# A four-layer graph network: the attention stage on pairs of tiles, with the cast and the subtract moved between GpSimd and VectorE

## The chip, the core and the metric

One core of one Trainium2 chip runs the whole program in one launch. The metric is the device time of that launch in microseconds. The profile names the engines: PE (TensorE matmul), PEld (its weight loads), DVE (VectorE), ACT (ScalarE), POOL (GpSimd), SP (the queue that issues most transfers).

## The reference

x is 4096 x 128 and adj 4096 x 4096, of zeros and ones and symmetric, both float32. Four layers follow one another, each on `h = relu(layernorm(x))` and added to x:

```
layer 0: dis = clip(adj.sum(1), 1) ** -0.5
         diffusion = (dis[:, None] * adj * dis[None, :]) @ h - h
         sim  = (h @ h.T) / (norms[:, None] * norms[None, :])
         attn = softmax(beta * sim * adj, axis=1)
         out  = diffusion + sigmoid(alpha) * (attn @ h - h)
layer 1: out = (1 / (adj.sum(1) + beta))[:, None] * (adj @ h + beta[:, None] * h) @ kernel + bias
layer 2: out = relu(D (adj + I) D (h @ W) + b),  D = (adj.sum(1) + 1) ** -0.5
layer 3: hyperbolic maps around adj @ log_map_zero(h_mul(h, embed) + bias) and a product with layer
```

## The kernel before

Precision is kept by splitting a float32 value into two float16 parts, high (a cast) and low (the value minus its high part); a product then takes three matmuls (high x high, high x low, low x high). Rows are taken in 32 blocks of 128 and in 8 chunks of 4 blocks (512 rows). Each engine has its own instruction stream, written out by hand; semaphores join them. What an engine does next is fixed by the order in its stream.

**Start, to about 60 us.** x is normed, split and transposed into `u_t`, the rows divided by their norms. Meanwhile SP loads adj in 64 halves of 1 MB (`load_half`, L244) into the two buffers of `stage`, ACT casts each half in two quarters to bytes and sums the degrees on the way (`cast_quarter`, L436), and SP transposes the bytes into `adj_t` (`turn_half`, L251). A load waits for the cast that frees its buffer and stands behind that half's transpose in SP's queue.

**Attention stage, to about 485 us.** For each chunk c of 512 query rows and each block s of 128 keys there is one tile of 128 x 512 scores, 256 tiles in all. A tile goes around all engines:

1. PE, `scores` (L1138): three matmuls into bank s % 4 of `ps_s`.
2. DVE, `z_step` (L755): times the adj bytes, in place in PSUM.
3. ACT, `exp_step` (L482): exp into `ez[s % 4]` in SBUF, float32.
4. DVE, `high_part` (L762): cast to float16, the high part.
5. POOL, `low_part` (L331): `ez` minus the high part, the low part.
6. PE, `att_products` (L1152): twelve matmuls of 129 columns that add attn @ h and the row sums of attn to the accumulators in `ps_acc`.

PE computes the scores of tile s + 4 ahead of the products of tile s. DVE's stream has the mask product one tile ahead of the cast, ACT's has the casts of the next chunk's halves between the exps at the steps of `CAST_AT`, in the first 24 of a chunk's 32 steps. At a chunk's end `att_tail` (L768 to L774) divides by the row sums and adds to x from the accumulators in PSUM; PE's first products of the next chunk wait for it (`acc_free`). `degrees` (L783 to L788) adds up the degree parts of the chunk, and POOL's `root_degree` (L288) raises them to -1/2. `x_minus_h` (L713) takes the h terms off x. Chunk 7 also holds the first half of the preparation of layer 0's aggregation, `hd = h * dis` with its split (`sum_hd` L794 and `low_hd` L801 on DVE, `high_hd` on ACT), and four quarters of the aggregation itself on PE. The chunk loops of all engines are hardware loops over a body of 32 steps.

**Layers, to the end.** PE multiplies split h by adj_t (`aggregate`, L1210): a quarter is eight matmuls of 512 columns, eight quarters make a chunk of 512 rows. At places named in `W_AFTER`, `T_AFTER` and `V_AFTER`, counted in quarters, it puts in small steps for a finished chunk. In layer 0 these are `weights` (L1239, four transposes of the result), `turn_h` (L1266, eight matmuls that transpose the new h) and `prepare` (L1275, its product with kernel). DVE adds prepare's result, times beta / (degree + beta), to x: this is layer 1's beta term. DVE's `split_h` (L881, L883) splits each chunk of the new h, and in layer 0 POOL adds the bias to x beside it (L368).

## Time and profile before

| | |
|---|---|
| Median of three runs | 1005.23 us (1004.9 to 1006.45) |
| The profiled execution's own time | 1004.54 us, its span 1002.7 us |
| Busy: PE, DVE, ACT, POOL | 894.8, 696.5, 517.2, 435.6 us |
| Mean granted clock of TensorE | 0.986 of full speed |
| Moved by DMA over the span | 89.33 MB, nearly all in the first 425 us |
| Share of the DMA engines, 200 to 250 us | 0.69, at 201 GB/s |

The busy times are read against the span: an engine that is full in one part of the program and idle in another shows a middling share. PE is near full in both halves. A PE busy time is not PE at its peak, since matmuls are pipelined and their ends are modelled. DVE's busy time includes time in which an instruction has been issued and cannot run yet. The chain of waits is the path that ended last, and a group's row gives, behind the bar, its busy time in all, the mean of one instruction and the idle time ahead of it.

### The profile page before, as it was taken

The page shows a single profiled execution, that of the slowest core. Times are in us where ns is not written, and L with a number is a line of the kernel's source. Part 1 is how long each engine was busy: PE and PEld are TensorE (multiplying, and loading weights), DVE is VectorE, ACT ScalarE, POOL GpSimd, SP SyncE. Part 2 cuts the span into 40 slices and gives each one's busy share as a digit, 9 for nine tenths or more (in the row PEclk, how much of TensorE's full clock was granted, in tenths as well). Part 3 has the DMA queues.
Part 4 walks back from the last instruction along what each step waited for, and adds up shares of the span by engine and source line. Part 5 has one row for each costly group of instructions (what it writes and reads, how often), then busy time and mean ns, then how long its engine had stood idle before and what let it go on. Part 6 is the DMA issues. An engine that isn't in the chain of part 4 may idle for free.

```text
span 1002.7 us, 20218 instructions
## 1 busy us (share of the span) xinstructions
PE 894.8 (89%) x6528; PEld 505.2 (50%) x6528; DVE 696.5 (69%) x1902; ACT 517.2 (52%) x1124; POOL 435.6 (43%) x380
## 2 busy tenths in 40 slices
PE   0188899989898989988999999999999999999992
PEld 0155555656555556555555545444445555545551
DVE  5988999999999999998434342232204766764767
ACT  4878686968686878656312211111105466435334
POOL 3677777777777787767311221000002222212221
PEclk9999999999999999999999999999999999999997
DMA  7979494948484858300000000000000000000100
GB/s 229 276 222 255 124 275 128 268 147 261 133 251 148 257 153 240 94 2 2 1 1 1 1 1 1 1 1 1 1 1 1 1 1 1 1 0 2 42 21 23
DMA packets 84784, 89.33 MB, mean 89 GB/s; under 512 B 71296, under 2 KB 76544, under 8 KB 76544
## 3 DMA queue, kind: packets, MB, share of 16 engines
q1 hardware_dynamic: 81088, 88.09, 30.0%
q10 hardware_dynamic: 3648, 0.61, 0.3%
q8 instruction: 29, 0.48, 0.2%
q14 instruction: 19, 0.16, 0.1%
HBM read 69.81 MB, written 2.10 MB: 72 GB/s over the span
## 4 chain that ended last, share of the span: by engine, by line
PE 28%; POOL 27%; issue 21%; DVE 16%; DVEq 3%; ACT 3%; DMA 1%; POOLq 1%; ACTq 0%; SPq 0%
POOL e_parts L331 23%; PE ps_acc L1210 19%; PE ps_t L1210 3%; DVE e_parts L762 2%; POOL hyp L359 2%; PE ps_s L1278 1%; DVE ez L685 1%; ACT ez L524 1%; PE ps_s L1241 1%; DVE h_a L883 1%; PE ps_t L1266 1%; DMA x<-in_x 1%; PE ps_s L1275 1%; POOL small L288 1%; ACT e_parts L555 1%
## 5 line engine op out<-in xcount | busy, mean ns | idle before, releaser
L331 POOL TENSOR_TENSOR e_parts<-ez,e_parts 128x512 f16<-128x512 f32 x256 | 303.1, 1186 | 110.1 <-DVE e_parts L762 110.1
L1152 PE MATMUL ps_acc<-h_a,e_parts 128*128 128x129 f16 x3072 | 223.7, 222 | 39.8 <-POOL e_parts L331 19.3
L1152 PEld LDWEIGHTS ps_acc<-h_a,e_parts 128*128 128x128 f16 x3072 | 183.4, 98 | 150.4 <-POOL e_parts L331 90.6
L482 ACT ACTIVATE ez<-ps_s,scal 128x512 f32<-128x512 f32 x256 | 196.4, 772 | 101.4 <-DVE ps_s L755 101.1
L762 DVE CAST e_parts<-ez 128x512 f16<-128x512 f32 x256 | 231.8, 905 | 10.8 <-ACT ez L482 10.1
L1138 PE MATMUL ps_s<-u_t 128*128 (+1 forms) x768 | 211.7, 386 | 0.0
L1210 PE MATMUL ps_acc<-adj_t,stage 128*128 128x512 fp8e4 x896 | 199.9, 379 | 0.0
L755 DVE TENSOR_TENSOR ps_s<-ps_s,adj_t 128x512 f32<-128x512 f32 x256 | 176.1, 688 | 2.9 <-issue 1.5
L1210 PE MATMUL ps_acc<-adj_t,h_a 128*128 128x512 fp8e4 x768 | 169.3, 379 | 0.0
L436 ACT ACTIVATE bytes<-stage 128x1024 uint8<-128x1024 f32 x128 | 134.1, 1048 | 9.5 <-DMA stage<-in_adj 9.2
L1210 PEld LDWEIGHTS ps_acc<-adj_t,stage 128*128 128x128 f16 x896 | 86.9, 98 | 97.5
L288 POOL TENSOR_TENSOR small<-small,scal 128x4 f32<-128x4 f32 x24 | 25.4, 1057 | 222.9 <-DVE small L865 222.9
L524 ACT ACTIVATE ez<-x,small 128x128 f32 (+1 forms) x96 | 39.5, 482 | 155.7 <-DVE small L877 155.7
L1210 PEld LDWEIGHTS ps_acc<-adj_t,h_a 128*128 128x128 f16 x768 | 75.0, 98 | 86.7
L852 DVE SCALAR_TENSOR_TENSOR x<-ps_s,cols,x 128x128 f32 x96 | 27.0, 345 | 101.2 <-PE ps_s L1241 51.0
L359 POOL TENSOR_TENSOR hyp<-hyp,scal 128x4 f32<-128x4 f32 (+1 forms) x37 | 39.3, 1063 | 132.7 <-ACT e_parts L555 119.3
L1138 PEld LDWEIGHTS ps_s<-u_t 128*128 128x128 f16 x768 | 66.3, 99 | 33.3 <-issue 3.9
L1210 PE MATMUL ps_t<-adj_t,h_a 128*128 128x512 fp8e4 x256 | 56.7, 379 | 0.0
L1125 PE MATMUL ps_s<-ident,adj_t 128*128 128x128 f16 x64 | 8.3, 310 | 48.1 <-POOL adj_t L301 47.9
L516 ACT ACTIVATE ez<-ps_acc 128x512 f32<-128x512 f32 x26 | 15.3, 590 | 69.4 <-PE ps_acc L1210 69.4
L1210 PEld LDWEIGHTS ps_t<-adj_t,h_a 128*128 128x128 f16 x256 | 25.0, 98 | 29.2
L288 POOL TENSOR_TENSOR cols<-cols,scal 128x4 f32 (+3 forms) x13 | 21.9, 1688 | 24.4 <-DVE cols L668 12.7
(159 smaller groups left out, 751.6 us busy)
## 6 DMA issues: line engine op xcount, KB each, us to landing
stage<-in_adj SPq DMA_DIRECT2D x64, 1024.0 KB, 5.2
x<-in_x SPq DMA_DIRECT2D x4, 512.0 KB, 9.8
out<-x SPq DMA_DIRECT2D x8, 256.0 KB, 2.1
adj_t<-bytes SPq DMA_TRANSPOSE x64, 3.1
kernel_sb<-in_L_gnn_kernel ACTq DMA_DIRECT2D x1, 64.0 KB, 6.6
w_sb<-in_L_gnn_W ACTq DMA_DIRECT2D x1, 64.0 KB, 7.3
embed_top<-in_L_gnn_embed ACTq DMA_DIRECT2D x1, 64.0 KB, 7.9
embed_top<-in_L_gnn_layer ACTq DMA_DIRECT2D x1, 64.0 KB, 6.8
```

The lines of the kernel that those rows point to most:

```text
L288: return g.tensor_tensor(col, col, e.broadcast_to(col.shape), ALU.pow)
L331: g.tensor_tensor(e_parts[:, LO, s % RING, :], ez[:, s % RING, :], e_parts[:, HI, s % RING, :], ALU.subtract).then_inc(elo_done, 1)
L359: g.tensor_tensor(dst, src, half.broadcast_to(dst.shape), ALU.pow).then_inc(done, 1)
L436: last = a.activation(bytes8[:, m % 2, cut], stage[:, m % 2, cut], ACT.Copy, scale=A_BYTE, accum_out=deg_parts[:, ds(BC * i + b, 1), 2 * h ...
L482: a.activation(ez[:, s % RING, :], ps_s[:, s % RING, :], ACT.Exp, scale=beta_s, bias=shift_c).then_inc(exp_done, 1)
L524: last = a.activation(hf[:, b, :], x[:, ds(BC * m + b, 1), :] .rearrange("p a f -> p (a f)"), ACT.Relu, bias=nb[:, b:b + 1], scale=rs[:, b ...
L755: v.tensor_tensor(ps_s[:, s % RING, :], ps_s[:, s % RING, :], adj_u8[:, k // 2, col, k % 2], ALU.mult).then_inc(z_done, 1)
L762: v.tensor_copy(e_parts[:, HI, s % RING, :], ez[:, s % RING, :]).then_inc(ehi_done, 1)
L852: v.scalar_tensor_tensor(xb, src[:, b, :], col[:, ds(BC * m + b, 1)], xb, ALU.mult, ALU.add)
L1138: last = t.matmul(ps_s[:, s % RING, :], u_t[:, rj, P * k:P * (k + 1)], u_t[:, ri, col], start=(n == 0), stop=(n == 2))
L1152: last = t.matmul(att_acc[:, b, 0:D + 1], e_parts[:, re, s % RING, P * b:P * (b + 1)], h_a[:, s, rh, 0:D + 1], start=(s == 0 and n == 0 an ...
L1210: last = t.matmul(acc, h[:, k, r, :], adj_f8[:, k // 2, CW * c:CW * (c + 1), k % 2], start=(k == 0 and r == LO), stop=(k == NB - 1 and r = ...
```

## The change

- The stage goes by pairs of tiles. `scores` fills a pair of PSUM banks, one of three pairs (`ps_t` is the third), six tiles ahead of the products. `z_pair` (L756) is one DVE instruction of 1024 columns, `exp_pair` (L480) one ACT instruction of 1024.
- The high part is cast by POOL (`high_part`, L332), the low part subtracted by DVE (`low_part`, L762). The ring of four tiles in `ez` and `e_parts` stays.
- At a chunk's end DVE copies the accumulators to `att_sb` in SBUF (`att_evac`, L768), frees them, and does the tail from there one pair later.
- ACT casts one quarter of adj behind each exp pair, 12 quarters ahead; six halves instead of eight are cast ahead of the stage. The mask product waits for half a chunk of transposes at a time.
- The chunk loops of PE, DVE, ACT and POOL in this stage are written out.
- Layer 1's beta term is added by PE: ACT and DVE make 128 x 128 diagonals of 2 beta in two float16 parts, and PE adds twelve matmuls of 128 columns per chunk to layer 1's aggregation. `turn_h` and `prepare` leave layer 0, and so does DVE's update of x with their result.

```diff
+BANKS = 3
+CAST_AHEAD = 12
+SUM_AT = [7, 9, 11, 13]
+HD_AT = [8, 10, 12, 14]
+LOW_AT = [9, 11, 13, 15]
-T_AFTER = ([w + 6 for w in W_0], (), [20, 25, 36, 41, 52, 57, 68, 73], ())
+T_AFTER = ((), (), [20, 25, 36, 41, 52, 57, 68, 73], ())
...
+        score_banks = (ps_s[:, 0:2, :], ps_s[:, 2:4, :], ps_t[:, :, :])
...
-            def low_part(s, base):
-                pool.wait_ge(ehi_done, base + s + 1)
-                g.tensor_tensor(e_parts[:, LO, s % RING, :], ez[:, s % RING, :],
-                                e_parts[:, HI, s % RING, :], ALU.subtract).then_inc(elo_done, 1)
-            def root_degree(i):
-                pool.wait_ge(pow_in, i + 1)
-                power(dis[:, ds(BC * i, BC)], neg_half).then_inc(pow_ok, 1)
-            with pool.Fori(0, NCH - 1) as i:
+            def high_part(g_s):
+                if g_s % 2 == 0:
+                    pool.wait_ge(exp_done, g_s // 2 + 1)
+                if g_s >= RING:
+                    pool.wait_ge(e_used, g_s - RING + 1)
+                g.tensor_copy(e_parts[:, HI, g_s % RING, :], ez[:, g_s % RING, :]
+                              ).then_inc(ehi_done, 1)
+            def root_degree(c):
+                pool.wait_ge(pow_in, c + 1)
+                power(dis[:, BC * c:BC * (c + 1)], neg_half).then_inc(pow_ok, 1)
+            for c in range(NCH):
                 for s in range(NB):
-                    low_part(s, NB * i)
-                    if s == 20:
-                        root_degree(i)
-            for s in range(NB):
-                low_part(s, NB * (NCH - 1))
-                if s == 6:
-                    root_degree(NCH - 1)
+                    high_part(NB * c + s)
+                    if s == (13 if c == NCH - 1 else 19):
...
+            def cast_quarter(n):
+                h, r = n // 2, n % 2
+                rows, hh = h // HPC * BC + h % BC, h % HPC // BC
                 if r == 0:
...
+            def exp_pair(p):
+                act.wait_ge(z_done, p + 1)
+                if p >= 2:
+                    act.wait_ge(elo_done, 2 * p - 2)
+                at = 2 * p % RING
+                a.activation(ez[:, at:at + 2, :], score_banks[p % BANKS], ACT.Exp, scale=beta_s,
                              bias=shift_c).then_inc(exp_done, 1)
             act.wait_ge(col_ok, 1)
...
+            for p in range(PAIRS):
+                exp_pair(p)
+                if p + CAST_AHEAD < PAIRS:
+                    cast_quarter(p + CAST_AHEAD)
+                if p // NP == NCH - 1 and p % NP in HD_AT:
+                    high_hd(HD_AT.index(p % NP))
...
+            def diag_high(m):
+                for b in range(BC):
+                    k = ds(BC * m + b, 1)
+                    last = a.activation(diag[:, HI, k, :].rearrange("p a f -> p (a f)"), ident32,
+                                        ACT.Copy, scale=beta2[:, k])
+                last.then_inc(diag_hi, 1)
             def layer0_chunk(m, bank):
                 agg_evac(m, bank)
                 relu_chunk(m, m)
-                ht_evac(m)
+                diag_high(m)
...
+            def z_pair(p):
+                c, k = p // NP, p % NP
+                if k % (NP // 2) == 0:
+                    for at in adj_turned:
+                        dve.wait_ge(at, 16 * (BC * c + BC // 2 * (1 + k // (NP // 2))))
+                dve.wait_ge(s_done, p + 1)
+                pair = score_banks[p % BANKS]
+                v.tensor_tensor(pair, pair, adj_u8[:, k, CW * c:CW * (c + 1), :]
+                                .rearrange("p i t -> p t i"), ALU.mult).then_inc(z_done, 1)
+            def low_part(g_s):
+                dve.wait_ge(ehi_done, g_s + 1)
+                v.tensor_tensor(e_parts[:, LO, g_s % RING, :], ez[:, g_s % RING, :],
+                                e_parts[:, HI, g_s % RING, :], ALU.subtract).then_inc(elo_done, 1)
+            def att_evac(c):
+                dve.wait_ge(e_used, NB * (c + 1))
+                v.tensor_copy(att_sb[:, :, :], att_acc[:, :, 0:D + 1]).then_inc(acc_free, 1)
+                dve.drain()
+            def att_tail(c):
+                v.reciprocal(rec, att_sb[:, :, D])
                 dve.drain()
                 v.tensor_scalar(rec, rec, sig_h, None, ALU.mult)
                 dve.drain()
                 for b in range(BC):
+                    xb = x[:, BC * c + b, :]
+                    v.scalar_tensor_tensor(xb, att_sb[:, b, 0:D], rec[:, b:b + 1], xb,
+                                           ALU.mult, ALU.add)
+                dve.drain()
+            def degrees(c):
...
+            z_pair(0)
+            z_pair(1)
+            for p in range(PAIRS):
+                c, k = p // NP, p % NP
+                if p + 2 < PAIRS:
+                    z_pair(p + 2)
+                low_part(2 * p)
+                low_part(2 * p + 1)
+                if c and k == 0:
+                    att_evac(c - 1)
+                if c and k == 1:
+                    att_tail(c - 1)
+                if c < NCH - 1 and k == 3:
+                    x_minus_h(slice(2 * c, 2 * c + 2), slice(BC * c, BC * (c + 1)))
+                if k == (5 if c == NCH - 1 else 8):
+                    degrees(c)
+                if c == NCH - 1:
+                    if k == SUM_AT[0]:
+                        for at in adj_turned:
+                            dve.wait_ge(at, 16 * BC * NCH)
+                    if k in LOW_AT:
+                        low_hd(LOW_AT.index(k))
+                        dve.drain()
+                    if k in SUM_AT:
+                        sum_hd(SUM_AT.index(k))
             rest = range(len(HD_AT), NCH)
             for m in rest[:2]:
                 sum_hd(m)
+            att_evac(NCH - 1)
...
-                dve.wait_ge(prep_done, m + 1)
-                dve.wait_ge(bias_in, m + 1)
-                update_x(inv_beta, prep_out, m)
+                dve.wait_ge(diag_hi, m + 1)
+                for b in range(BC):
+                    k = ds(BC * m + b, 1)
+                    last = v.scalar_tensor_tensor(diag[:, LO, k, :].rearrange("p a f -> p (a f)"),
+                                                  ident32, beta2[:, k],
+                                                  diag[:, HI, k, :].rearrange("p a f -> p (a f)"),
+                                                  ALU.mult, ALU.subtract)
+                last.then_inc(diag_ok, 1)
...
+            def scores(g_s):
+                p, c, k = g_s // 2, g_s // NB, g_s % NB
+                if g_s % 2 == 0 and p >= BANKS:
+                    pe.wait_ge(exp_done, p - BANKS + 1)
                 for n, (rj, ri) in enumerate(((HI, HI), (HI, LO), (LO, HI))):
+                    last = t.matmul(score_banks[p % BANKS][:, g_s % 2, :],
+                                    u_t[:, rj, P * k:P * (k + 1)],
+                                    u_t[:, ri, CW * c:CW * (c + 1)], start=(n == 0), stop=(n == 2))
+                if g_s % 2:
+                    last.then_inc(s_done, 1)
+            def att_products(g_s):
+                c, s = g_s // NB, g_s % NB
+                if c == 0 and s % BC == 0:
                     pe.wait_ge(split0_ok, s // BC + 1)
+                if c and s == 0:
+                    pe.wait_ge(acc_free, c)
+                pe.wait_ge(elo_done, g_s + 1)
...
+                last.then_inc(e_used, 1)
...
+            for g_s in range(2 * BANKS):
+                if g_s < 2:
+                    pe.wait_ge(ut_ok, 5 + g_s)
+                elif g_s < 4:
+                    pe.wait_ge(ut_last_ok, g_s - 1)
+                scores(g_s)
+            for g_s in range(NB * (NCH - 1)):
+                scores(g_s + 2 * BANKS)
+                att_products(g_s)
...
+                if L == 1 and q == NB // BC - 1:
+                    pe.wait_ge(diag_ok, c + 1)
+                    for b in range(BC):
+                        for rh, rd in ((HI, HI), (HI, LO), (LO, HI)):
+                            t.matmul(acc[:, P * b:P * (b + 1)], h[:, BC * c + b, rh, :],
+                                     diag[:, rd, BC * c + b, :], start=False, stop=False,
+                                     skip_group_check=True)
```

DVE's stream at the end of chunk 0, before:

```order
L755 TENSOR_TENSOR ps_s<-ps_s,adj_t 128x512
L759 REGISTER_ALU
L762 CAST e_parts<-ez 128x512 [waits e_used,exp_done]
L755 REGISTER_ALU [waits s_done]
L755 TENSOR_TENSOR ps_s<-ps_s,adj_t 128x512
L759 REGISTER_ALU
L762 CAST e_parts<-ez 128x512 [waits e_used,exp_done]
L767 ISA
L768 RECIPROCAL small<-ps_acc 128x4 [waits e_used]
L770 TENSOR_SCALAR small<-small,scal 128x4
L774 SCALAR_TENSOR_TENSOR x<-ps_acc,small,x 128x128
```

and now (the names behind "waits" are semaphores):

```order
L756 TENSOR_TENSOR ps_s<-ps_s,adj_t 128x1024 [waits s_done]
L762 TENSOR_TENSOR e_parts<-ez,e_parts 128x512 [waits ehi_done] x2
L768 COPY att_sb<-ps_acc 128x516 [waits e_used]
L756 TENSOR_TENSOR ps_s<-ps_s,adj_t 128x1024 [waits s_done]
L762 TENSOR_TENSOR e_parts<-ez,e_parts 128x512 [waits ehi_done] x2
L773 RECIPROCAL small<-att_sb 128x4
L775 TENSOR_SCALAR small<-small,scal 128x4
L779 SCALAR_TENSOR_TENSOR x<-att_sb,small,x 128x128 x4
L756 TENSOR_TENSOR ps_t<-ps_t,adj_t 128x1024 [waits s_done]
L762 TENSOR_TENSOR e_parts<-ez,e_parts 128x512 [waits ehi_done] x2
```

The mask product and the subtracts come by pairs, the subtracts wait for POOL alone, and the copy of the accumulators stands behind the first subtracts of the next chunk, with the arithmetic on them one pair later.

PE's stream in layer 0, the small steps around chunk 1, before:

```order
L1239 MATMUL ps_s<-ident_sb,ez 128x128 [waits agg_out]
L1239 MATMUL ps_s<-ident_sb,ez 128x128 x3
L1210 MATMUL ps_acc<-adj_t,stage 128x512 [waits acc_free]
L1210 MATMUL ps_acc<-adj_t,stage 128x512 x47
L1266 MATMUL ps_t<-ident,h_a 128x128 [waits l_split]
L1266 MATMUL ps_t<-ident,h_a 128x128 x7
L1210 MATMUL ps_acc<-adj_t,stage 128x512 x8
L1239 MATMUL ps_s<-ident_sb,ez 128x128 [waits l_stats,agg_out]
L1239 MATMUL ps_s<-ident_sb,ez 128x128 x3
L1275 MATMUL ps_s<-kernel_sb,bytes 128x128 [waits ht_out]
L1275 MATMUL ps_s<-kernel_sb,bytes 128x128 x3
L1210 MATMUL ps_acc<-adj_t,stage 128x512 x8
```

and now at the end of chunk 0 in layer 1, where the diagonals come in:

```order
L1233 MATMUL ps_acc<-adj_t,h_a 128x512 x7
L1233 MATMUL ps_acc<-adj_t,h_a 128x512 [waits l_split]
L1233 MATMUL ps_acc<-adj_t,h_a 128x512 x7
L1221 MATMUL ps_acc<-u_t,h_a 128x128 [waits diag_ok,l_split]
L1221 MATMUL ps_acc<-u_t,h_a 128x128 x11
L1233 MATMUL ps_acc<-adj_t,h_a 128x512 x8
L1221 MATMUL ps_acc<-u_t,h_a 128x128 [waits diag_ok,l_split]
L1221 MATMUL ps_acc<-u_t,h_a 128x128 x11
L1233 MATMUL ps_acc<-adj_t,h_a 128x512 x8
```

The transposes and the kernel product have gone out of layer 0, and twelve products come in ahead of the last quarter of each chunk of layer 1.

## Rows read from the trace of the kernel before

**Rows 1.** Waits, all engines: waiting line, releaser: us in total, times, longest.
```profile
POOL e_parts L331 <- DVE e_parts L762: 110.1, 236, 2.3
...
PEld ps_t L1266 <- DVE h_a L883: 3.9, 7, 0.6
```

**Rows 2.** Chain that ended last, middle of chunk 3: start us, us, what.
```profile
228.29 1.16 POOL e_parts L331
...
229.82 1.15 POOL e_parts L331
```

**Rows 3.** The same chain over the whole span, its longest pieces.
```profile
224.82 1.60 POOL e_parts L331
...
276.96 1.60 POOL e_parts L331
...
485.27 20.72 PE ps_t L1210 x96
```

**Rows 4.** Groups by line and form, DVE: xcount | busy us, mean ns | idle before.
```profile
L762 DVE CAST e_parts<-ez 128x512 f16<-128x512 f32 x256 | 231.8, 905 | 10.8 <-ACT ez L482 10.1
L755 DVE TENSOR_TENSOR ps_s<-ps_s,adj_t 128x512 f32<-128x512 f32 x256 | 176.1, 688 | 2.9 <-issue 1.5 <-PE ps_s L1138 1.4
...
L883 DVE TENSOR_TENSOR e_parts<-ez,e_parts 128x512 f16<-128x512 f32 x8 | 5.5, 692 | 0.6
```

**Rows 5.** Timeline in order of time, all engines, layer 0: start us, us, instruction [idle before].
```profile
542.67 1.51 POOL L368 TENSOR_TENSOR x<-x,bias_bc 128x512 f32 x1 [2.44 <-ACT ez L524]
543.22 1.51 DVE L883 TENSOR_TENSOR h_a<-ez,h_a 128x512 f32 x1 [0.16 <-issue]
```

**Rows 6.** The same view in the last attention chunk.
```profile
445.67 0.68 DVE L801 TENSOR_TENSOR stage<-bytes,stage 128x512 f16<-128x512 f32 x1
445.83 1.53 POOL L331 TENSOR_TENSOR e_parts<-ez,e_parts 128x512 f16<-128x512 f32 x1 [0.36 <-DVE e_parts L762]
...
446.27 0.68 DVE L755 TENSOR_TENSOR ps_s<-ps_s,adj_t 128x512 f32<-128x512 f32 x1
```

**Rows 7.** Groups by line and form, POOL.
```profile
L279 POOL TENSOR_SCALAR_AFFINE_SELECT ident<-ident 128x128 f16<-128x128 f16 x1 | 0.3, 293 | 0.2 <-POOL ident_sb L276 0.2
...
L274 POOL MEMSET ident<- 128x128 f16 x1 | 0.2, 204 | 0.3 <-POOLq L1311 0.3
...
L281 POOL MEMSET scal<- 128x1 f32 x1 | 0.1, 99 | 0.0
```

**Rows 8.** Timeline of PE in attention steps, each released without a wait.
```profile
256.80 0.85 PE L1152 MATMUL ps_acc<-h_a,e_parts 128*128 128x129 f16 x12
...
258.14 0.85 PE L1152 MATMUL ps_acc<-h_a,e_parts 128*128 128x129 f16 x12
```

**Rows 9.** Timeline of PE: first attention step, first step of chunk 1.
```profile
61.45 0.86 PE L1152 MATMUL ps_acc<-h_a,e_parts 128*128 128x129 f16 x12
...
115.95 1.03 PE L1152 MATMUL ps_acc<-h_a,e_parts 128*128 128x129 f16 x12 [2.24 <-DVE x L774]
```

**Rows 10.** Groups by line and form, ACT.
```profile
L482 ACT ACTIVATE ez<-ps_s,scal 128x512 f32<-128x512 f32 x256 | 196.4, 772 | 101.4 <-DVE ps_s L755 101.1
L436 ACT ACTIVATE bytes<-stage 128x1024 uint8<-128x1024 f32 x128 | 134.1, 1048 | 9.5 <-DMA stage<-in_adj 9.2
L524 ACT ACTIVATE ez<-x,small 128x128 f32 x80 | 33.0, 482 | 127.8 <-DVE small L877 127.8
```

**Rows 11.** Timelines of SP's queue and of ACT around one load.
```profile
230.89 1.23 SPq L251 DMA_TRANSPOSE adj_t<-bytes  x1
232.16 0.58 SPq L244 DMA_DIRECT2D stage<-in_adj  x1
...
237.44 1.06 ACT L436 ACTIVATE bytes<-stage 128x1024 uint8<-128x1024 f32 x1 [0.20 <-DMA stage<-in_adj]
```

**Rows 12.** Timeline of weight loads (PEld), layer 0, chunk 2.
```profile
544.78 0.45 PEld L1266 LDWEIGHTS ps_t<-ident,h_a 128*128 128x128 f16 x8 [0.58 <-DVE h_a L883]
...
547.30 0.97 PEld L1275 LDWEIGHTS ps_s<-kernel_sb,bytes 128*128 128x128 f32 x8
```

More of the change, by code:

```diff
@@ L41 @@
 RING = 4
-Z_AHEAD = 1
-EARLY = 2
-CAST_AT = [3 * m + r for m in range(HPC) for r in (1, 2)]
-HD_AT = [8 + 6 * m for m in range(4)]
+PAIRS = NP * NCH
+BANKS = 3
[3 more added lines that the diff above has]
+LOW_AT = [9, 11, 13, 15]
 FILL_AT = [27, 28, 29, 30]
@@ L230, in _ @@
         def _(sp):
[L232 to L235 removed]
+            for s in (w_done, l_split):
+                sp.sem_inc(s, 1)
             for n in range(NG):
@@ L425, in _, with cast_half @@
                           l1_beta.rearrange("(c p t) -> p c t", p=P, t=2)).then_inc(params_in, 16)
-            def cast_quarter(i, m, r):
-                hh, b = m // BC, m % BC
+            def cast_quarter(n):
+                h, r = n // 2, n % 2
+                rows, hh = h // HPC * BC + h % BC, h % HPC // BC
                 if r == 0:
-                    act.wait_ge(adj_in[m % 2], (HPC // 2 * i + m // 2 + 1) * 16)
-                    if type(i) is not int or HPC * i + m >= 2:
-                        act.wait_ge(adj_turned[m % 2], (HPC // 2 * i + m // 2) * 16)
+                    act.wait_ge(adj_in[h % 2], (h // 2 + 1) * 16)
+                    if h >= 2:
+                        act.wait_ge(adj_turned[h % 2], (h // 2) * 16)
                 cut = slice(HALF // 2 * r, HALF // 2 * (r + 1))
-                last = a.activation(bytes8[:, m % 2, cut], stage[:, m % 2, cut], ACT.Copy,
+                last = a.activation(bytes8[:, h % 2, cut], stage[:, h % 2, cut], ACT.Copy,
                                     scale=A_BYTE,
-                                    accum_out=deg_parts[:, ds(BC * i + b, 1), 2 * hh + r])
+                                    accum_out=deg_parts[:, rows, 2 * hh + r:2 * hh + r + 1])
                 if r:
                     last.then_inc(cast_done, 1)
-            def cast_half(i, m):
+            def cast_half(h):
                 for r in range(2):
-                    cast_quarter(i, m, r)
+                    cast_quarter(2 * h + r)
             def relu_group(n):
@@ L503, in high_hd @@
                              ).then_inc(hd_hi, 1)
-            for s in range(NB):
-                exp_step(s, NB * (NCH - 1))
-                if s in HD_AT:
-                    high_hd(HD_AT.index(s))
+            for p in range(PAIRS):
[4 more added lines that the diff above has]
+                    high_hd(HD_AT.index(p % NP))
             for m in range(len(HD_AT), NCH):
@@ L613, in _ @@
             i = NCH // 2 - 1
-            ht_evac(2 * NCH - 1)
+            ht_evac(NCH - 1)
             ln_step(2 * i + 1)
@@ L772, in att_tail @@
                 for b in range(BC):
[L773 to L782 removed]
+                    xb = x[:, BC * c + b, :]
[3 more added lines that the diff above has]
+            def degrees(c):
+                cut = slice(BC * c, BC * (c + 1))
+                dve.wait_ge(cast_done, HPC * (c + 1))
                 v.tensor_reduce(deg[:, cut], deg_parts[:, cut, :], mybir.AxisListType.X,
@@ L1157, in att_products @@
                                         skip_group_check=True)
-                return last
-            for s in range(RING):
-                if s < 2:
-                    pe.wait_ge(ut_ok, 5 + s)
-                else:
-                    pe.wait_ge(ut_last_ok, s - 1)
-                scores(s, 0, slice(0, CW))
-            with pe.Fori(0, NCH - 1) as i:
-                for s in range(NB):
-                    s_s = s + RING
-                    scores(s_s, NB * i, ds(CW * (i + s_s // NB), CW))
-                    att_products(s, NB * i, i).then_inc(e_used, 1)
+                last.then_inc(e_used, 1)
[8 more added lines that the diff above has]
+                att_products(g_s)
             def aggregate(L, c, q):
@@ L1215, in aggregate @@
                     last.then_inc(agg_done, 1)
-            base = NB * (NCH - 1)
-            for s in range(NB):
-                if s + RING < NB:
-                    scores(s + RING, base, slice(CW * (NCH - 1), N))
-                att_products(s, base, NCH - 1).then_inc(e_used, 1)
-                if s in FILL_AT:
-                    aggregate(0, *QUARTERS_0[FILL_AT.index(s)])
+            for g_s in range(NB * (NCH - 1), NB * NCH):
+                if g_s + 2 * BANKS < NB * NCH:
+                    scores(g_s + 2 * BANKS)
+                att_products(g_s)
+                if g_s % NB in FILL_AT:
+                    aggregate(0, *QUARTERS_0[FILL_AT.index(g_s % NB)])
             pe.wait_ge(params_in, 16 * N_PARAMS)
```

135 lines of the change are left out of this document (30 added, 105 removed).

## Prediction

> **What bounds the kernel now.** The page's forty slices show PE near nine tenths in two regimes: in the first half DVE is as full, and POOL nearly so; in the second half PE stands alone. So I read the waits first. The largest of the attention stage is POOL's: its subtract on L331 waits 110 us in all for the DVE cast on L762 [rows 1]. The chain of waits then gives the beat of the stage. In the middle of a chunk it runs through POOL alone, one subtract of 1.16 us every 1.53 us [rows 2]. Equal places of two chunks lie 52.14 us apart [rows 3]. 32 beats of 1.53 are 48.9 us, so about 3.3 us of a chunk are its tail, when the accumulators are read and PE stands still.
>
> Why is the beat 1.53 when the subtract takes 1.16? The DVE groups tell: the cast shows a mean of 905 ns, the mask product a steady 688, and a subtract like POOL's done by DVE with no POOL work beside it 692 [rows 4]. The cast is on record while it waits: it cannot run until POOL's subtract is over, and POOL cannot begin before the cast. The two take turns, 1.16 + 0.37.
>
> **The same turn-taking after the change.** The cast goes to POOL and the subtract to DVE, so it matters whether these also exclude one another. Layer 0 has this pair: a DVE subtract from two SBUF tiles that is issued beside a POOL instruction takes 1.51 us instead of 0.69, and ends 0.55 after it [rows 5]. The other way round, a DVE sum of two SBUF tiles, running from 445.67, stretches the POOL subtract that starts 0.16 later to 1.53, 0.37 more than its 1.16; DVE's next instruction starts 0.60 after the sum [rows 6]. The port seems to come free some 0.14 before an instruction's recorded end. That is by itself a case against this change: one shared turn is exchanged for another, and DVE's part of it grows from about 0.37 to 0.55. The Trainium skill, page SBUF — State Buffer, section Who interferes with whom, says the same: a VectorE instruction with two SBUF inputs contends with a GpSimd instruction that reads SBUF. By that rule, the trace agrees. Without the exclusion the sum below would end at PE's own rate, 925 us; with it, at 938.
>
> **POOL's cast.** The trace has no cast on POOL; I call its time c. Above it stands the subtract, 1.16, which reads two tiles where a cast reads one. Nearer from above: AFFINE_SELECT reads one tile and computes, 293 ns at 128 columns. From below: MEMSET only writes, 204 ns at 128 columns and 99 at one [rows 7]. By columns these give for 512: 0.10 + 512 x 1.53 ns = 0.88, and 0.10 + 512 x 0.83 ns = 0.52. I take the middle of the two, c = 0.70, as a cast reads and writes once and computes next to nothing. The Trainium skill, page GPSIMD Engine Reference, section 3.1, gives 769 ns for a 512-element loop; no run here shows it. An estimate by that page would be c = 0.77, and the sum 949 us.
>
> **DVE and POOL per pair of tiles.** The mask product on two tiles lies between 0.69 and twice that; 512 columns more are read in about 0.55, the time DVE took from when the port came free [rows 5], so I take 0.69 + 0.55 = 1.24, or 1.15 until the next can start (neighbours overlap by 0.09, as 0.69 against 0.60 in [rows 6]). Beside it POOL casts, and holds the port for 2c - 0.14 = 1.26. Then DVE subtracts twice, 2 x 0.60. A pair so takes max(1.15, 1.26) + 1.20 = 2.46, against 2 x 1.53 = 3.06 before. Sixteen pairs are 39.4.
> DVE's other work per chunk: the 3.3 of the tail now, which stays (degrees, reciprocal, x updates); the copy of 516 accumulator columns out of PSUM, which I price as a mask product, 0.7; and 0.8 because the x updates now read two SBUF tiles and can each be held up by a cast. Together 4.8. Chunk by this bound: 39.4 + 4.8 = 44.2.
>
> **PE.** Its step, three score products and twelve for the sum, takes 258.14 - 256.80 = 1.34 when nothing is late [rows 8], so 42.9 a chunk. The 2.24 us that it stands idle at a chunk's start, and the slow step behind it, [rows 9] mostly go: it waits only until the copy is out, has six tiles of scores in three bank pairs instead of four ahead, and I leave 0.5. Chunk by this bound: 43.4.
> Two bounds this close do not mesh without loss, with only four tiles in the ring. I add 0.8 to the larger: **45.0 per chunk**, against 52.14.
>
> **ACT and the loads** do not bind by this sum, narrowly. Exp grows by (772 - 482)/384 = 0.755 ns a column [rows 10], so on 1024 columns it takes 0.77 + 0.39 = 1.16; with one quarter cast, 1.05 and its accumulator read, some 2.2 per pair. For the loads, the loop of one buffer counts: SP starts the load 1.27 after the transpose, data are there 5.2 later, when ACT goes on [rows 11]. With the two quarters of a half now one pair P apart, the loop is P + 1.05 + 0.2 + 1.27 + 5.2 and has 4 pairs of time, so P must be at least 2.57. We need 2.8. If loads are late, exp stands behind the cast in ACT's order.
>
> **Layer 0.** The transposes of h (0.45) and the kernel product (0.97) leave PE: 8 x 1.42 = 11.4 us. So does the wait for DVE's split ahead of them [rows 12], 3.9 in all [rows 1]. Added are 12 products of 128 columns per chunk with the diagonals, at 0.45/8: 8 x 0.68 = 5.4, on PE too. Net 9.9. Building the diagonals goes beside PE on ACT and DVE, each idle over half of that layer. Only if they were late for the last quarter of a chunk in layer 1 would PE wait, and they are a layer early.
> Costing nothing: the unrolled loops (fewer register steps; PE's longer instruction stream must be fetched, and in the later layers, unrolled too, it runs without gaps), the load order, and six casts instead of eight ahead of the stage.
>
> **The sum.** The stage runs from 61.45 [rows 9] to 485.27 [rows 3]: 423.8 us. Six chunks at 52.14 are 312.8; the first and last are 111.0 together. After: 6 x 45.0 = 270.0; the first 45.5; the last 51.0, since it carries four quarters of aggregation (32 products at 20.72/96 us [rows 3], 6.9 us of PE) and the sums and splits of hd (eight at 0.68 [rows 6], 5.4 us of DVE). That is a gain of 57.3. The start is 0.8 later, as the first exp needs two tiles. Gain in all: 57.3 - 0.8 + 9.9 = 66.4. The profiled execution took 1004.5 us, 0.7 below the median of the three runs: **938 us**. In general, with y for a chunk, the gain is 426.4 - 8y.
>
> **Rivals.**
> 1. *POOL's cast is no faster than its subtract*, and the change does not do what it says. With c = 1.16 a pair is 2.18 + 1.20 = 3.38, a chunk 54.1 + 4.8 = 58.9, the time 1049 us: **slower**. It decides from c = 0.99 (y = 53.3). For it: a third of the subtract's time may be fixed cost or the output's conversion. Against it: the one-input row of 293 ns. Chance 0.10.
> 2. *The cast is only somewhat faster*, c from 0.82 to 0.97; at 0.88 y = 49.9 and the time is 977. Chance 0.15.
> 3. *PE becomes the bound outright*, with c at 0.6 or less, or with turns that mesh well: y = 43.4, the time 925. For it: PE's 1.34 needs only the ring kept full. Chance 0.13.
> 4. *Loads become the bound.* They now run through the whole chunk. If a landing takes 6.5 instead of 5.2, P is 3.0, a chunk 49, the time 970. For it: ACT waited for one already [rows 11]. Against: that was in a burst, eight halves in 24 steps or one per 4.6 us, and now one comes each 5.6. Chance 0.08.
> 5. *Gains and losses cancel*, c near 0.98: chance 0.02.
>
> **How the numbers follow.** The forecast's own case, c from 0.6 to 0.8, has 0.52, and gives 926 to 957. The range for 8 in 10 takes in rivals 2 to 4: 922 to 980. What is left out is rival 1, rival 5 and the upper edge of 2. Two runs of this kernel can be told apart from about 0.2%, or 2 us. Faster: 0.52 + 0.13 + 0.15 + 0.08 = 0.88, of which I give 0.01 away to no change. Same 0.03, slower 0.10.
>
> **What would show it.** Right: POOL's cast group with a mean under about 0.9, its least time 0.7; DVE's two-tile product at 1.24; DVE's subtract mean above its 0.69, between 0.75 and 1.1, since it waits on record; chunks 44 to 46 us apart; PE full in the stage and its idle at a chunk's start under 1 us; layer 0 without the two small groups and about 10 us shorter. Wrong: a cast at 1 us or more, where the chain again alternates POOL and DVE; a DVE subtract at 0.69 flat, where there is no exclusion and PE leads; many waits of ACT for stage, where loads lead; gaps of PE at no semaphore, where the fetch of instructions costs what I put at nothing.

## The result: 1052.8 us, slower by 4.8%

The changed kernel takes 1052.78 us (median of 4 runs, 1051.77 to 1055.63) beside 1005.07 (median of 4 runs) for the kernel before on the same chip: ratio 1.048, 95% interval 1.046 to 1.050. The prediction said 938 and faster, with 922 to 980 as its range. It was wrong in sign and by 115 us.

**The page.** PE's busy time, and the slices of PE and DVE:
```profile
PE 878.0 (83%) x6496; PEld 507.0 (48%) x6496; DVE 673.4 (64%) x1782; ACT 486.2 (46%) x1020; POOL 315.0 (30%) x380
...
PE   0287777787877777787799999999999999999992
...
DVE  6988777787877778787863444133213567764757
```
The loss is in the attention stage, and there no engine is full any longer: PE and DVE both stand at seven to eight tenths, where before both were near nine. One stretch in numbers (columns: us, busy us and instructions of PE, PEld, DVE, ACT, POOL, granted clock, DMA share, GB/s):
```profile
200.00:250.00 50.00, 38.44 (x406) 25.26 (x404) 40.10 (x51) 30.61 (x42) 21.18 (x29) 1.00 0.60 171
```
When nobody is full, somebody waits for everybody: read the waits.

**Waits**, all engines (waiting line, releaser: us in total, times, longest); [rows 1] held this view before:
```profile
POOL e_parts L332 <- ACT ez L480: 237.2, 103, 5.8
...
ACT ez L480 <- DVE e_parts L762: 181.4, 119, 4.0
...
PEld ps_acc L1167 <- DVE e_parts L762: 138.9, 112, 2.2
PE ps_acc L1167 <- DVE e_parts L762: 91.9, 117, 1.7
...
DVE ps_s L756 <- PE ps_s L1150: 63.4, 79, 2.5
```
POOL waits for ACT, ACT and PE for DVE's subtract, and DVE's mask product for PE's scores. A circle of waits, and the chain says which one. **The chain that ended last**, middle of the stage (start us, us, what), against [rows 2]:
```profile
252.19 1.23 DVE ps_s L756
253.43 0.85 DVE e_parts L762
254.27 0.05 issue
254.32 0.86 PE ps_acc L1167 x12
255.18 0.66 PE ps_s L1150 x3
255.84 0.02 issue
255.87 1.23 DVE ps_s L756
```
The same four pieces come again and again: mask product 1.23, first subtract 0.85, the products with e 0.86, one tile of scores 0.66. With gaps of 0.08 that is 3.68 us for a pair of tiles, 3.06 before. The orders of two streams close this circle. Write g for a tile and p for a pair, tiles 2p and 2p + 1, and att(g) for the products with e of tile g. PE issues scores(g + 6) and then att(g), so scores(2p + 7) stands behind att(2p). Att(2p) waits for subtract(2p). DVE issues z_pair(p + 2) ahead of both subtracts of pair p; z_pair(p + 3) needs scores(2p + 7), its second tile, and subtract(2p + 2) stands behind it. So from one first subtract to the next lie one att, one tile of scores, one two-tile mask product, whatever the banks hold.

**Groups by line and form**, for [rows 4, 7, 10]:
```profile
L762 DVE TENSOR_TENSOR e_parts<-ez,e_parts 128x512 f16<-128x512 f32 x256 | 209.9, 858 | 2.7 <-POOL e_parts L332 2.7
...
L332 POOL CAST e_parts<-ez 128x512 f16<-128x512 f32 x256 | 183.2, 742 | 274.2 <-ACT ez L480 237.2 <-PE ps_acc L1167 37.0
...
L756 DVE TENSOR_TENSOR ps_s<-ps_s,adj_t 128x1024 f32<-128x1024 f32 x86 | 105.9, 1232 | 63.8 <-PE ps_s L1150 63.4
L480 ACT ACTIVATE ez<-ps_s,scal 128x1024 f32<-128x1024 f32 x86 | 103.4, 1203 | 128.1 <-DVE e_parts L762 120.7 <-DVE ps_s L756 7.4
```
POOL's cast has a least and median time of 607 and 613 ns, cheaper than I had forecast; its mean of 742 holds waits for the port, the SBUF port that POOL shares with DVE. The other durations of the stage came as forecast. The parts are right; their order is what costs.

**Later layers.** From the end of the attention stage (541.09, before 485.27 [rows 3]) to the end of the span are 510.6 us, before 517.4: 6.8 less, which goes with the exchange of transposes for diagonals (e4 below runs that part alone). So all up to the end of the stage lost 55.8.

### The profile page after: what moved, and what is told of

It is laid out like the page before. It is cut to its first block, busy times and chain, and to the rows that moved or that the text cites. A ratio compares the mean times of both kernels' runs of the same rounds, so it can differ in the third digit from the quotient of the medians.

```text
span 1051.7 us, 18224 instructions
## 1 busy us (share of the span) xinstructions
PE 878.0 (83%) x6496; PEld 507.0 (48%) x6496; DVE 673.4 (64%) x1782; ACT 486.2 (46%) x1020; POOL 315.0 (30%) x380
## 4 chain that ended last, share of the span: by engine, by line
PE 49%; DVE 34%; issue 8%; DVEq 4%; POOL 2%; ACT 1%; DMA 1%; ACTq 0%; POOLq 0%; SPq 0%
PE ps_acc L1233 24%; PE ps_acc L1167 10%; DVE ps_s L756 10%; DVE e_parts L762 8%; PE ps_s L1150 5%; DVE ps_t L756 5%; PE ps_t L1233 3%; PE ps_t L1150 3%; POOL att_sb L356 2%; PE ps_s L1294 1%; DVE ez L689 1%; PE ps_s L1262 1%; DMA x<-in_x 1%; ACT e_parts L559 1%; DVEq L789 1%
## 5 line engine op out<-in xcount | busy, mean ns | idle before, releaser
L332 POOL CAST e_parts<-ez 128x512 f16<-128x512 f32 x256 | 183.2, 742 | 274.2 <-ACT ez L480 237.2
L762 DVE TENSOR_TENSOR e_parts<-ez,e_parts 128x512 f16<-128x512 f32 x256 | 209.9, 858 | 2.7 <-POOL e_parts L332 2.7
L480 ACT ACTIVATE ez<-ps_s,scal 128x1024 f32<-128x1024 f32 x86 | 103.4, 1203 | 128.1 <-DVE e_parts L762 120.7
L756 DVE TENSOR_TENSOR ps_s<-ps_s,adj_t 128x1024 f32<-128x1024 f32 x86 | 105.9, 1232 | 63.8 <-PE ps_s L1150 63.4
L1150 PE MATMUL ps_s<-u_t 128*128 128x512 f16 x516 | 142.5, 387 | 0.0
L356 POOL TENSOR_TENSOR att_sb<-att_sb,scal 128x4 f32<-128x4 f32 (+1 forms) x37 | 39.4, 1065 | 132.9 <-ACT e_parts L559 119.3
L480 ACT ACTIVATE ez<-ps_t,scal 128x1024 f32<-128x1024 f32 x42 | 50.5, 1204 | 60.7 <-DVE e_parts L762 60.7
L756 DVE TENSOR_TENSOR ps_t<-ps_t,adj_t 128x1024 f32<-128x1024 f32 x42 | 51.8, 1232 | 30.1 <-PE ps_t L1150 29.8
L1150 PE MATMUL ps_t<-u_t 128*128 128x512 f16 x252 | 69.2, 384 | 0.0
L1150 PEld LDWEIGHTS ps_s<-u_t 128*128 128x128 f16 x516 | 44.7, 99 | 23.4 <-issue 3.5
```

The costliest lines, as they stand in the source:

```text
L332: g.tensor_copy(e_parts[:, HI, g_s % RING, :], ez[:, g_s % RING, :]).then_inc(ehi_done, 1)
L356: g.tensor_tensor(dst, src, half.broadcast_to(dst.shape), ALU.pow).then_inc(done, 1)
L480: a.activation(ez[:, at:at + 2, :], score_banks[p % BANKS], ACT.Exp, scale=beta_s, bias=shift_c).then_inc(exp_done, 1)
L756: v.tensor_tensor(pair, pair, adj_u8[:, k, CW * c:CW * (c + 1), :] .rearrange("p i t -> p t i"), ALU.mult).then_inc(z_done, 1)
L762: v.tensor_tensor(e_parts[:, LO, g_s % RING, :], ez[:, g_s % RING, :], e_parts[:, HI, g_s % RING, :], ALU.subtract).then_inc(elo_done, 1)
L1150: last = t.matmul(score_banks[p % BANKS][:, g_s % 2, :], u_t[:, rj, P * k:P * (k + 1)], u_t[:, ri, CW * c:CW * (c + 1)], start=(n == 0), s ...
```

## The experiments

Three theories stood at the start. A: the circle through the order of the two streams. B: DVE and POOL take turns at their port, and this stretches the subtracts. C: the ring of four tiles of e is too short. Twelve kernels ran in three groups, each group on another chip: e1 to e4, e5 to e8, e9 to e12. The kernel before ran beside each group, with medians of 1004.76, 1005.29 and 1005.98, and every ratio below is to that median; across groups, compare the ratios.

**e1: PE computes both score tiles first.**
```
-for g_s: scores(g_s + 6); att_products(g_s)
+for g_s in steps of 2:
+    scores(g_s + 6); scores(g_s + 7); att_products(g_s); att_products(g_s + 1)
```


> Edit: PE's stream has both score tiles of a pair ahead of both products of a pair; nothing else. Theory A (a loop through the order of two streams): in the changed kernel one pair takes 3.5 to 3.7 us because the second score tile stands behind the products that wait for DVE's first subtract, and the next two-tile mask product stands ahead of the next subtracts. With the order turned the loop spans two pairs, and a pair falls to about 2.8 us (DVE's own 1.15 + 2 x 0.7, or PE's 2.68): time 950 to 975 us. Theory B (turns at the port between POOL's cast and DVE's subtract set the pace): the work at the port is unchanged, time within 5 us of 1053. Theory C (the ring of four tiles: exp waits for the subtracts of two pairs back): as B.

Measured 962.65, ratio 0.959 (0.957 to 0.960). No work was removed, and 90 us are gone: theory A. The turns at the port have not become cheaper (subtract's mean 867, cast's 901), so it is not theory B that gained them. In the middle of a chunk the chain runs through DVE alone now:
```profile
261.94 1.23 DVE ps_s L756
263.17 1.35 DVE e_parts L762 x2
264.52 1.14 DVE ps_t L756
```

**e2: DVE makes the mask product behind the two subtracts.**
```
-z_pair(p + 2); low_part(2 * p); low_part(2 * p + 1)
+low_part(2 * p); low_part(2 * p + 1); z_pair(p + 2)
```


> Edit: DVE's stream has the mask product of pair p + 2 behind the two subtracts of pair p instead of ahead of them. Theory A: this opens the same loop at its other end, since the subtracts no longer stand behind a mask product that waits for PE: 950 to 985 us. Theory B: no change of the work at the port, 1053 within 5. Theory C: exp gets its scores later, so 1053 or slower.

Measured 940.70, ratio 0.937 (0.935 to 0.938). The 950 to 985 of theory A was too slow; in the middle of a chunk PE leads, at the 1.34 a tile of [rows 8]:
```profile
254.23 0.65 PE ps_s L1150 x3
254.87 0.69 PE ps_acc L1167 x12
```
e2 is better than e1, and the timelines show a reason. In the changed kernel and in e1 the exp of a pair waits for subtracts that stand behind the mask product, so in many pairs the casts start just ahead of the next subtracts and the four share the port (first fence, the changed kernel; second, e1). In e2 the casts run beside the mask product, which doesn't lengthen them: two take 1.18 (third fence, e2).
```profile
274.76 1.63 POOL L332 CAST e_parts<-ez 128x512 f16<-128x512 f32 x2 [1.91 <-ACT ez L480]
...
275.13 1.80 DVE L762 TENSOR_TENSOR e_parts<-ez,e_parts 128x512 f16<-128x512 f32 x2
```
```profile
265.58 1.69 DVE L762 TENSOR_TENSOR e_parts<-ez,e_parts 128x512 f16<-128x512 f32 x2
...
265.88 1.86 POOL L332 CAST e_parts<-ez 128x512 f16<-128x512 f32 x2 [2.50 <-ACT ez L480]
```
```profile
254.93 1.22 DVE L756 TENSOR_TENSOR ps_s<-ps_s,adj_t 128x1024 f32<-128x1024 f32 x1
255.02 1.18 POOL L332 CAST e_parts<-ez 128x512 f16<-128x512 f32 x2 [1.16 <-ACT ez L480]
...
256.06 1.28 DVE L762 TENSOR_TENSOR e_parts<-ez,e_parts 128x512 f16<-128x512 f32 x2
```

**e3: POOL writes a constant in place of the cast.**
```
-g.tensor_copy(e_parts[:, HI, slot, :], ez[:, slot, :])
+g.memset(e_parts[:, HI, slot, :], 1.0)
```


> Edit: POOL's cast is replaced by a memset of the same tile (the high part is then a constant; the attention result is left out of what is computed). POOL still writes 512 columns but reads nothing. Theory B: the turns at the port are gone, DVE's subtract falls to 0.69 in each case and a pair to about 2.7: 940 to 970 us. Theory A: only the 0.15 to 0.25 that the first subtract of a pair is stretched by leaves the loop, 128 pairs: 1020 to 1035 us. Theory C: exp to exp over two pairs loses the stretch only, as A.

The kernel leaves out the cast; the subtract makes exp minus 1 as the low part, so attention is still computed, at lower precision. Measured 1029.05, ratio 1.024 (1.022 to 1.026). The turns are gone, each subtract takes 0.60 in the chain, and the circle stays:
```profile
251.92 1.23 DVE ps_t L755
253.16 0.60 DVE e_parts L761
253.76 0.05 issue
253.80 0.86 PE ps_acc L1166 x12
254.66 0.66 PE ps_s L1149 x3
255.33 0.02 issue
255.35 1.23 DVE ps_s L755
```
3.43 us a pair in place of 3.68: 0.25 x 128 pairs is 32 us, 23.7 were measured over the whole; not every first subtract of the changed kernel is stretched to 0.85. Turn-taking is worth that much of the changed kernel's time; it is not what made it slow.

**e4: the diagonals alone, on the kernel before.**
```
-transposes of h (L1266) and kernel product (L1275) in layer 0
+diag_high on ACT, its low part on DVE, 12 products a chunk in layer 1
```


> Edit: the kernel before with the beta part of the change alone (diagonals, no transposes of h and no kernel product in layer 0; the attention stage as before). All theories: the prediction's term of 9.9 us; the spans of the changed kernel from the end of attention (541.1 to 1051.7 against 485.3 to 1002.7) give 6.8. So 995 to 999 us.

Measured 997.73, ratio 0.993 (0.991 to 0.995): 7.0 us faster.

**e5: the accumulators copied out ahead of the mask product**, on e2.
```
 low_part(2 * p); low_part(2 * p + 1)
+if c and k == 0: att_evac(c - 1)
 z_pair(p + 2)
-if c and k == 0: att_evac(c - 1)
```


> The kernel with the mask product behind the two subtracts (940.7 us), and at a chunk's start the copy of the accumulators ahead of that mask product instead of behind it. There TensorE stands still for 2.5 us at each of seven boundaries (17.6 us in the two groups whose releaser is the copy's result), and 46.16 us a chunk stand against the 42.9 of its products alone. If the copy is late because the mask product of 1.23 stands ahead of it, each boundary gives 1.2 us back: 7 x 1.2 = 8.4, and the time is 931 to 934 us. Rival: the boundary is lost to the loads or to the exp instructions behind the ACT casts, and the copy's place is worth nothing: 939 to 942.

Measured 941.19, ratio 0.936 (0.935 to 0.938): nothing gained, as its rival had it. PE's wait for the copy falls from 7.1 us to 1.1, and its wait for the subtracts rises from 10.4 to 14.6. My reading of e2's waits was wrong. The 17.6 adds PE's own 7.1 and the 10.5 of its weight loads, which are largely the same stretches, so PE stands still for 1.0 at a boundary, not 2.5; and which of DVE's results it waits for there is a matter of order.

**e6: cast back on DVE, subtract back on POOL**, on e2, the cast on two tiles at once.
```
-POOL: tensor_copy(high); DVE: subtract, subtract, z_pair
+POOL: subtract, tile by tile; DVE: tensor_copy(high, 128 x 1024), z_pair
```


> The kernel with the mask product behind the subtracts (940.7 us), with the two engines' work put back: VectorE casts the pair in one instruction and GpSimd subtracts tile by tile. If moving the cast to GpSimd is what lets TensorE lead, GpSimd's two subtracts (2 x 1.16) and the turn of the pair's cast in between (0.37 for one tile before, some 0.7 for two) bound a pair at 2.9 to 3.05 against 2.68 now: 16 x 8 x 0.22 to 0.37 more, 970 to 990 us. If the swap bought nothing and two-tile instructions alone did it, the time stays within 938 to 950.

Measured 969.34, ratio 0.965 (0.963 to 0.967). That is just under the 970 to 990 that was expected if the division matters. The largest part of the chain goes through POOL:
```profile
266.12 0.70 DVE e_parts L764
266.83 0.07 issue
266.89 2.72 POOL e_parts L330 x2
```
With the mask product where e2 has it, cast and subtract moved as in e2 are worth 28.6 us against this. Not all of that need be the division of the work: here POOL's first subtract also waits for a cast of two tiles, and DVE's mask product waits 55 us in all for scores. The old division with a cast tile by tile in this order was not run.

**e7: constant in place of the cast**, on e1 (the high part is 1, as in e3).

> The kernel with both score tiles ahead of the products with e (962.7 us, VectorE leads at 2.75 us a pair), with GpSimd writing a constant (no reading) in place of its cast; the low part, exp minus the high part, carries the rest. If in that kernel VectorE's subtracts are lengthened by taking turns with GpSimd's reads, the pair falls to TensorE's own 2.68 or near it, and the subtract's mean from 0.80 toward 0.69: 935 to 950 us. If turn-taking costs nothing there and the order of VectorE's work alone sets 2.75, the time stays at 958 to 964.

Measured 931.51, ratio 0.927 (0.925 to 0.928), 31 us less than e1 and below the 935 to 950 expected. The subtract's mean falls from 867 to 682. With no reads of POOL at the port, PE leads:
```profile
247.94 1.29 PE ps_t L1149 x6
249.23 1.52 PE ps_acc L1166 x24
```
So theory B holds for e1, the kernel with the circle open: there the turns are what holds DVE above PE's rate.

**e8: the swap alone, on the kernel before**, tile by tile, POOL's chunk loop written out.
```
-DVE: tensor_copy(high);   POOL: tensor_tensor(low, subtract)
+POOL: tensor_copy(high);  DVE: tensor_tensor(low, subtract)
```


> The kernel before (1004.8 us) with nothing changed but who casts and who subtracts, tile by tile; GpSimd's loop over the chunks is written out. Its streams have no circle such as the changed kernel's: the mask product of one tile waits for scores that were computed four products earlier. GpSimd needs 0.61 a tile instead of 1.16, VectorE 0.60 + 0.69 = 1.3 and up to 0.2 of turns; by the order z, subtract, z, subtract, two tiles take 0.69 + 0.77 + 0.61 + 0.69 and three gaps, some 2.9 us. So 1.35 to 1.48 us a tile against 1.53: 960 to 990 us, faster. If the turn-taking itself is what the swap buys or loses, and both directions cost the same, 1000 to 1010.

Measured 998.14, ratio 0.994 (0.992 to 0.996): 7 us, where 15 to 45 were expected, or nothing if the turns alone counted; it lies between the two. The timeline:
```profile
253.48 0.69 DVE L756 TENSOR_TENSOR ps_s<-ps_s,adj_t 128x512 f32<-128x512 f32 x1
...
254.21 0.78 ACT L483 ACTIVATE ez<-ps_s,scal 128x512 f32<-128x512 f32 x1 [0.93 <-DVE ps_s L756]
...
255.05 0.62 POOL L332 CAST e_parts<-ez 128x512 f16<-128x512 f32 x1 [1.01 <-ACT ez L483]
...
255.70 0.69 DVE L761 TENSOR_TENSOR e_parts<-ez,e_parts 128x512 f16<-128x512 f32 x1 [0.33 <-POOL e_parts L332]
```
Mask product, exp, cast and subtract of one tile follow each other without a gap, and with the mask product only one tile ahead this chain of 2.9 us bounds two tiles; ACT's casts of 1.05 come between. POOL's casts start at 241.10 and, 14 later, at 261.90: 1.49 us each, against 1.53. My reading is that the swap needs the mask product further ahead to pay; no run tried that with single tiles.

**e9: DVE's boundary work spread out**, on e2.
```
-k == 1: reciprocal and four x updates;  k == 3: x_minus_h
+k == 2: reciprocal;  k == 3..6: one x update each;  k == 7, 9: half of x_minus_h each
```


> The kernel with the mask product behind the subtracts (940.7 us), with VectorE's extra work at a chunk's start taken apart: the reciprocal at pair 2, the four x updates one each at pairs 3 to 6, the other update of x as two halves at pairs 7 and 9. Moving the copy alone changed nothing (941.2): TensorE then waited for the subtracts instead, since VectorE as a whole is late there. VectorE has 2.34 us of work in a pair of 2.68, so it makes up 0.34 a pair. If the lump is what costs the 3.3 us a chunk over TensorE's 42.9, spreading it gives back up to that, 7 x 1 to 2.5: 923 to 934 us. Rival: VectorE's total is the limit (16 x 2.34 and 5 to 6 us of other work are 43 to 44 a chunk and the turns come on top), so the spread gives nothing: 938 to 942.

Measured 936.70, ratio 0.931 (0.929 to 0.933): 4 us less than e2 (by the ratios 6), between the 923 to 934 expected and the rival's 938 to 942. The lump costs a little. The 3.3 us a chunk that the expectation set out from includes 1.0 of last-chunk aggregation, so there were 2.3 to gain. What holds the rest, DVE's total or the loads (ACT waits 33.4 us for them here, 23.8 in e2), was not separated.

**e10: e9 with e1's order on PE.**

> As the kernel with the spread tail, and TensorE computes both score tiles of a pair ahead of the products with e of two tiles. The mask product is then never behind TensorE's products, but TensorE asks for two tiles of e at once. Within 0.3% of the kernel with the spread tail if the circle is already open there; 4 us or more faster if the remaining waits of VectorE for scores matter; slower if the ring of four tiles is now the limit.

Measured 939.73, ratio 0.933 (0.931 to 0.935). The intervals of e9 and e10 overlap: no difference shown.

**e11: e10 with the load ahead of the transpose in SP's queue.**
```
-turn_half(n); load_half(n + 2)
+load_half(n + 2); turn_half(n)
```


> As the kernel before this one in the list, and SP issues the next load ahead of the transpose (1.27 us). ACT waits for loads 24 us in all where the mask product stands behind the subtracts, in 26 places. If those waits reach TensorE, 2 to 8 us faster; if ACT's slack (39 of 50 us busy) hides them, the same within 0.2%; slower if transposes then come late for the mask product.

Measured 934.75, ratio 0.928 (0.926 to 0.930), the fastest kernel here that computes all of it at full precision, 7% below the kernel before. Its interval overlaps e9's, but neither e10's, from which it differs by the one edit, nor e2's (0.935 to 0.938). So the edit gave some 5 us, within the 2 to 8 expected. ACT's waits moved more than they shrank: 37.4 us for loads in e10, here 1.0 for loads and 33.3 for the transposes that free its byte buffers.

**e12: the changed kernel with the mask product tile by tile.**
```
-z_pair(p + 2); low_part(2 * p); low_part(2 * p + 1)
+z_tile(2 * p + 4); low_part(2 * p); z_tile(2 * p + 5); low_part(2 * p + 1)
```


> The changed kernel (1052.8 us) with one edit: the mask product is made tile by tile, in the order mask, subtract, mask, subtract; exp stays on two tiles. If the circle closes because one mask product needs both score tiles and stands ahead of both subtracts, it is open here: the second tile's mask product waits for scores that stand ahead of the products two tiles back. VectorE then has four instructions of 0.60 and some turn-taking, 2.4 to 2.8 a pair: 935 to 965 us. If the circle theory is wrong and turn-taking or the exp pair sets 3.6, it stays at 1040 or more.

Measured 952.39, ratio 0.946 (0.944 to 0.948). The chain is DVE's four instructions of about 0.6:
```profile
257.18 0.61 DVE ps_s L757
257.79 0.59 DVE e_parts L763
```
This edit adds an instruction a pair and gains 100 us. It shows how the circle closes: one instruction that takes two tiles waits for the later one and holds up what stands behind it. Note that the edit does two things, it splits the mask product and sets the second half behind the first subtract. Split alone, with both halves ahead of both subtracts, the walk still comes back through scores(2p + 7); that order was not run.

**The theories.** A is shown by e1, e2 and e12, three edits in different places that each open the same circle and leave all work in. B is a second-order cost (e3: 24 us, e7: 31 us). C falls: the ring is four tiles in all of them, and e2 runs at PE's rate. The written-out loops and their longer instruction streams are no cause either: e1 and e2 have them too.

## Why the prediction was wrong, step by step

**The step that failed is PE's**, the sentence "it waits only until the copy is out, has six tiles of scores in three bank pairs instead of four ahead", and the one that followed from it, "I add 0.8 to the larger". I had bounded each engine by its own work and counted buffers, and took what two close bounds lose for a small mesh loss. I never walked the streams: what stands behind what, and whether it leads back. Walked with numbers that the prediction had, a mask product of 1.24, a subtract of 0.60 and one step of PE of 1.34 are 3.18 a pair, already above the 2.46 and 2.68 of the two bounds and above the 3.06 of before. With the 4.8 of DVE's other work that is 55.7 a chunk, beyond the 53.3 at which the prediction's own formula turns to slower. In the trace the subtract is 0.85, as it shares the port, PE's step from rest is 0.86 + 0.66, and there are 0.08 of gaps: 3.68. Over a chunk, 59.3 was measured against the larger bound of 44.2: what was put at 0.8 is 15.1. The terms were at hand. No rival had it either: the one on the slower side needed a slow cast, and that its 1049 us lie near the measured time is chance.

**The sum was sound but for that term.** The distance of the copies L768 gives a chunk, less 6.9 for the last chunk's aggregation:

| kernel | first and last copy | y | 1004.5 - (426.4 - 8y) | measured |
|---|---|---|---|---|
| changed | 119.4, 541.1 | 59.26 | 1052.2 | 1052.8 |
| e1 | 106.5, 449.9 | 48.07 | 962.7 | 962.7 |
| e2 | 104.1, 427.2 | 45.17 | 939.5 | 940.7 |

Part of this agreement is cancellation: the formula holds 9.9 us for layer 0, where 7.0 were measured, and with 7.0 each row would come out 2.9 later. E2's chunk of 45.2 and its 940.7 us are near the 45.0 and 938 of the prediction. That is no merit of the prediction, since the change has another order in it, and luck besides: the cast was cheaper than forecast and the boundary dearer.

**POOL's cast.** Forecast 0.70 from bounds of 0.52 and 0.88, measured 0.61. E3's write of 512 columns takes 0.525, as the lower bound had it. The conditions of rivals 1, 2 and 5 fall. The Trainium skill, page GPSIMD Engine Reference, section 3.1, gives 769 ns for a tight loop over 512 elements and does not say that a cast is one; the trace does not agree with it as a price for the cast, which takes 613. The 949 us worked out from it leave out the 0.8 for meshing that the forecast's own sum has; with it they are 956. The times of rivals 1 and 2 leave it out too.

**The port.** That DVE's subtract and POOL's cast exclude one another is right: the subtract's mean is 858 ns, and 683 in e3, where POOL reads nothing. The rule of the Trainium skill, page SBUF — State Buffer, section Who interferes with whom, which excepts a GpSimd instruction that only writes, is borne out by the two means. But I priced it as a fixed turn per pair. How much is shared depends on whether the casts fall beside the mask product (e2: mean 753) or beside the subtracts (the changed kernel: 858).

**Two-tile instructions.** Mask product 1.23 (forecast 1.24), exp 1.20 (1.16), copy 0.68 (0.7): right. ACT's sum for a pair was short by a term that it names: exp 1.16, cast 1.05 and the accumulator read of 0.19 are 2.4, not 2.2, still less than a pair.

**PE's step and rival 3.** 1.34 when nothing is late: right, in e2. PE takes the lead there, as rival 3 said, but the boundary costs 45.2 - 42.9 = 2.3 a chunk and not 0.5.

**Loads, rival 4.** ACT waits for them 0.9 us in the changed kernel, as everything else is slow. At e2's pair of 2.68 it is 23.8, and 51.3 in e7: waits grow as the pair nears the bound of P = 2.57. No run got below 2.67 in the middle of a chunk, so the bound itself was not tested; e11, with the load issued first, is the one sign (5 us) that these waits reach PE.

**Layer 0.** Forecast 9.9, measured 7.0 in e4. The diagonals cost 0.67 a chunk in layer 1, as forecast:
```profile
721.76 0.67 PE ps_acc L1221 x12
722.43 3.45 PE ps_acc L1233 x16
725.88 0.89 PE ps_s L1262 x8
```
In layer 0 the chain of the kernel before has 0.62 for the transposes and 0.91 for the kernel product:
```profile
530.66 0.62 PE ps_t L1266 x8
531.28 1.73 PE ps_acc L1210 x8
533.45 0.91 PE ps_s L1275 x8
```
8 x 1.53 less 8 x 0.67 is 6.9, all of the gain. The 1.42 of the prediction were the times of the weight loads. The 3.9 that I added for their waits [rows 1, 12] was hardly any time of PE's. Where the weight loads of chunk 2 wait 0.58, PE multiplies until 544.70 and goes on at 544.78:

```profile
534.18 10.52 PE L1210 MATMUL ps_acc<-adj_t,stage 128*128 128x512 fp8e4 x48
544.78 0.62 PE L1266 MATMUL ps_t<-ident,h_a 128*128 128x128 f16 x8
```

## What to carry to other kernels

Bounds by engine and by buffer are necessary and not sufficient. Where several in-order streams feed each other, walk one round: for each instruction, what it waits for and what stands behind it; if the walk comes back to the same engine one round later, the sum of its durations is a bound of its own. Be most wary when two instructions are merged into one: the merged one waits for the later input and holds up everything behind it, so place it behind what the others wait for.

## What the runs showed that was not expected

The order of DVE's stream alone, one instruction moved behind two others (e2), takes this kernel from 1052.8 to 940.7 us, 11%, with the same instructions. And the parts of the change don't add: alone, the swap (e8) gives 7 us and the diagonals (e4) 7; the rest of the change in e2's order with the old division of cast and subtract, a two-tile cast and the diagonals included (e6), 36; all together in e2, 64, and in the order given, a loss of 48.
